# A fused attention and FFN kernel: score tiles of 32x64 without the masked quarter, and an output projection in fp16 halves scaled by a maximum that TensorE turns over

## The chip, the cores and the metric

The kernel runs on one core of a Trainium2 chip. The metric is the device time of one execution in microseconds (us), as the median of several runs. Five engines work side by side: TensorE (PE in the profile, its weight loads PEld), VectorE (DVE), ScalarE (ACT), GpSimd (POOL) and SyncE (SP), which issues the transfers.

## What is computed

x is (4, 2048, 512). Four layers stand one behind the other, each with a layernorm ahead and a residual added:

```
x = x + attention_a(layernorm(x))   # linear attention, 16 heads of 64, relu, cumulative sums
x = x + ffn(layernorm(x))           # int8-like: round rows and rhs, x @ rhs, scale back
x = x + attention_b(layernorm(x))   # gated, decaying linear attention, then layernorm
x = x + ffn(layernorm(x))           # the same rhs
```

attention_b, the second attention, is what the change is about:

```
q, k, v = x @ q_w.T, x @ k_w.T, x @ v_w.T      # 16 heads of 32; q and k then turned by rope
q_r, k_r = per head: q @ Wq[h].T, k @ Wk[h].T  # rank 16
g = sigmoid(x @ g_w.T + g_b)
M = M * decay + (g_t * k_t * scale) outer v_t  # M is 16 x 32 per head
y = q_t @ M
out = Y @ out_w.T + out_b;  hres = x + out;  layernorm(hres) * ln_g + ln_b
```

## The kernel before

The rows of x are worked in 64 chunks of 128 rows, in order. Within a chunk the recurrences are products: in attention_b the scores q·k of each pair of rows are formed, those with a key behind the query are multiplied by 0 (the mask `causals`), the rest is multiplied with v, and the state M of the chunks before is added.

Each chunk is cut into about 110 named units, each a few instructions of one engine. The table `ORDER` gives each unit a place and a lag: in slot s, every engine walks the table from top to bottom and does its own units, unit u for chunk s minus lag(u). So in one slot the units of five or six chunks stand between each other. The order is fixed in the program, an engine never skips a unit that has to wait, and units wait for each other through semaphores. The first slots are written out, the middle ones are a loop of two slots, the last are written out again (`run`, `walk`). `BANK` says which of the 8 PSUM banks a unit writes; before it writes, the unit waits until the unit that used the bank before has been read. `LATE` puts the preparation of weights into the first slots: load, maximum on DVE (`max`), turned by PE (`all`), power-of-two scale (`scale`), fp16 high half on ACT (`hi`), fp16 low half on DVE (`lo`). Semaphore counts inside the loop need registers; they are set by REGISTER_ALU instructions in the engine's own stream (`COUNTS`).

Products with fp32 accuracy are made in two ways. `three_pass` (L718 to L720) takes both operands as two fp16 halves and issues hi·hi, hi·lo, lo·hi. The others multiply fp32 tiles directly; the profile shows two MATMUL instructions for each such call. Small products use a part of the array: a product over 32 rows with 64 results takes a 32x64 tile of it, and calls that lie in different tiles can run beside each other.

The units of attention_b for one chunk, in the order of dependence: `xTb` (split and turn the normalised rows), `kb`, `qb`, `gb`, `vb` (projections), `kb_e`, `qb_e` and so on (rope, halves), `kr`, `qr` (rank products), `kr_e` (khat = kr times gate), `kT` and `kT_e` (turned, masked by head parity), `sb` (scores: L960, 16 calls, each 32 rows by 128 keys by 128 queries, 4 head groups l in 4 row groups of the array and 4 banks), `ys` (L970, q times state), `ub` (L996, state update), `sb_e0` and `sb_e1` (mask on DVE, L1434), `yb` (L983, scores times v), `y_e` (ACT copies y to SBUF, L1120), `out` (L1008, y times out_w in fp32, 4 calls of 128x128 by 512), `out_e` (L1447), `no_st`, `no_rs`, `no_ap`, `no_f` (layernorm, x3). The next chunk's `nb_ap` waits for `no_f`, since both use the tile xnb. Units of the first attention that matter here: `qk0` to `qk3` (projections, 48 fp16 matmuls each, L718 to L720), `s0`, `s1` (L800, scores in 64x64 tiles that already leave out a quarter), `so`, `o` (L818, L844), `u0`, `u1` (L863, in 128x64 tiles), `wo0`, `wo1`. The two FFNs are `mm0`, `mm1` (L891).

Of the kernel before, what the change touches and what calls it, by code (L numbers as in the profile page):

```python
# [59 lines left out]
ORDER = [("qr_e", 4), ("xhb", 4), ("sb", 4), ("ys", 4), ("mm1_e", 5), ("sb_e1", 4), ("qk2", 1), ("ub", 4), ("sb_e0", 4),  # L60
         ("mm1_a", 5), ("aT1_l", 2), ("qk1_e", 1), ("yb", 4), ("aT1_t", 2), ("u1", 2), ("y_e", 4), ("u0", 2),
         ("ub_e", 4), ("ld_t", 3), ("mm0_a", 3), ("u0_e", 2), ("nb_st", 3), ("nb_rs", 3), ("kt0", 1),
         ("bias", 2), ("u1_e", 2), ("out", 4), ("qk2_e", 1), ("wo0", 2), ("out_e", 4), ("no_st", 4),
         ("kt0_e", 1), ("wo1", 2), ("no_ap", 4), ("no_rs", 4), ("no_f", 4), ("nb_ap", 3), ("xTb_h", 3),
# [1504 lines left out]
```

## Time and profile before

| | |
|---|---|
| median of 3 runs | 3157.41 us (3151.66 to 3161.16) |
| the profiled execution | 3157.91 us, its span from first to last instruction 3156.2 us |
| PE busy | 3020.7 us, 96% |
| PEld busy | 2280.0 us, 72% |
| DVE busy | 2311.1 us, 73% |
| POOL, ACT busy | 997.9 us, 32%; 711.4 us, 23% |
| granted TensorE clock, mean | 0.987 |

The page of the profile gives for each engine its busy time, then the span in 40 slices with the busy share in tenths, then the chain of work that ended last. Views of the trace give more: the timeline lists instructions in order of time (several alike and consecutive are merged into one row with a count), the view by stretch gives the busy time of each engine between two points, the groups add up instructions of a line and shape. Matmuls are pipelined: the duration of one is a latency (0.22 us for 128 columns in fp16), and the next starts long before it ends (0.056 us later). What a matmul costs is therefore read from start to start.

### The profile page before, as it was taken

The numbers are of one execution on the slowest core, as the hardware profiler recorded it, in microseconds if no ns is written. First come the engines' busy times: TensorE is split into PE (matmuls) and PEld (weight loads), VectorE is DVE, ScalarE is ACT, GpSimd is POOL, SyncE is SP. The second block draws the span as 40 slices with busy tenths as digits, with TensorE's granted clock in tenths as the row PEclk, the third lists the DMA queues.
The fourth block names the chain that finished last, engine by engine and source line by source line (L and its number), as shares of the span: only waits on it lengthen the run. The fifth ranks groups of instructions, "written<-read, shape, count | busy, mean of one in ns | idle before, by whom it ended". The sixth has DMA issues, their size and how long they took to land.

```text
span 3156.2 us, 117197 instructions
## 1 busy us (share of the span) xinstructions
PE 3020.7 (96%) x50710; PEld 2280.0 (72%) x50836; DVE 2311.1 (73%) x5280; ACT 711.4 (23%) x1229; POOL 997.9 (32%) x1397
## 2 busy tenths in 40 slices
PE   3699999999999999999999999999999999999985
PEld 3577777777777777777777777777777777777764
DVE  6777777777777777777777777777777777777764
ACT  2222222222222222222122122222222222222211
POOL 2033333333333333333333333333333333333333
PEclk9899999999999999999999999999999999999997
DMA  4222222122222222222222222222222222222210
GB/s 169 67 41 47 45 47 51 38 48 51 37 48 51 41 44 51 42 44 50 44 47 44 44 47 45 45 46 45 45 46 46 50 40 48 50 37 48 50 34 27
DMA packets 384337, 152.96 MB, mean 48 GB/s; under 512 B 352800, under 2 KB 361632, under 8 KB 383904
## 3 DMA queue, kind: packets, MB, share of 16 engines
q1 hardware_dynamic: 383904, 146.02, 23.5%
q8 instruction: 414, 6.78, 0.9%
q14 instruction: 19, 0.16, 0.0%
HBM read 45.29 MB, written 16.78 MB: 20 GB/s over the span
## 4 chain that ended last, share of the span: by engine, by line
PE 94%; DVE 3%; DMA 1%; issue 1%; ACT 0%; POOL 0%; SPq 0%; DVEq 0%; POOLq 0%
PE bank L718 22%; PE bank L720 21%; PE bank L719 21%; PE bank L1008 7%; PE bank L891 3%; PE bank L844 3%; PE bank L800 3%; PE bank L676 3%; PE bank L960 2%; PE bank L818 2%; PE bank L863 2%; PE bank L983 2%; PE bank L970 1%; PE bank L996 1%; DVE absmax L1146 1%
## 5 line engine op out<-in xcount | busy, mean ns | idle before, releaser
L718 PE MATMUL bank<-xaT,wq_hi 128*128 128x128 f16 x2048 | 363.1, 221 | 5.0 <-DVE wk_lo L1171 4.0
L718 PE MATMUL bank<-xbT,wb 128*128 128x128 f16 x2048 | 350.7, 220 | 13.6 <-DMA xbT<-work 13.6
L719 PE MATMUL bank<-xaT,wq_hi 128*128 128x128 f16 x2048 | 362.6, 221 | 0.0
L720 PE MATMUL bank<-xaT,wq_lo 128*128 128x128 f16 x2048 | 362.6, 221 | 0.0
L718 PE MATMUL bank<-xaT,wk_hi 128*128 128x128 f16 x2048 | 360.3, 220 | 0.0
L719 PE MATMUL bank<-xaT,wk_hi 128*128 128x128 f16 x2048 | 360.1, 220 | 0.0
L720 PE MATMUL bank<-xaT,wk_lo 128*128 128x128 f16 x2048 | 360.0, 220 | 0.0
L719 PE MATMUL bank<-xbT,wb 128*128 128x128 f16 x2048 | 350.6, 220 | 0.0
L720 PE MATMUL bank<-xbT,wb 128*128 128x128 f16 x2048 | 350.6, 220 | 0.0
L638 POOL TENSOR_TENSOR work<-work 128x512 f32<-128x512 f32 x128 | 162.8, 1272 | 487.2 <-DVE work L1401 487.2
L1434 DVE TENSOR_TENSOR work<-bank,causal 128x512 f32<-128x512 f32 x256 | 159.0, 684 | 142.8 <-PE bank L960 142.8
L661 POOL TENSOR_TENSOR xf<-xwb,xf 128x512 f32<-128x512 f32 x64 | 80.9, 1264 | 528.5 <-DVE xf L1377 528.5
L1008 PE MATMUL bank<-wout,work 128*128 128x512 f32 x512 | 232.7, 597 | 1.2 <-ACT work L1120 1.2
L718 PEld LDWEIGHTS bank<-xaT,wq_hi 128*128 128x128 f16 x2048 | 202.6, 99 | 30.5 <-issue 14.7
L718 PEld LDWEIGHTS bank<-xbT,wb 128*128 128x128 f16 x2048 | 202.0, 99 | 22.2 <-DMA xbT<-work 9.8
L719 PEld LDWEIGHTS bank<-xaT,wq_hi 128*128 128x128 f16 x2048 | 202.7, 99 | 15.6
L719 PEld LDWEIGHTS bank<-xbT,wb 128*128 128x128 f16 x2048 | 202.0, 99 | 7.3
L720 PEld LDWEIGHTS bank<-xaT,wq_lo 128*128 128x128 f16 x2048 | 202.7, 99 | 0.0
L718 PEld LDWEIGHTS bank<-xaT,wk_hi 128*128 128x128 f16 x2048 | 202.0, 99 | 0.0
L720 PEld LDWEIGHTS bank<-xbT,wb 128*128 128x128 f16 x2048 | 202.0, 99 | 0.0
L719 PEld LDWEIGHTS bank<-xaT,wk_hi 128*128 128x128 f16 x2048 | 201.9, 99 | 0.0
L720 PEld LDWEIGHTS bank<-xaT,wk_lo 128*128 128x128 f16 x2048 | 201.9, 99 | 0.0
(207 smaller groups left out, 7928.1 us busy)
## 6 DMA issues: line engine op xcount, KB each, us to landing
xin<-in_L_attn_a_x SPq DMA_DIRECT2D x64, 256.0 KB, 2.6
out<-xf SPq DMA_DIRECT2D x64, 256.0 KB, 2.5
table<-in_tables SPq DMA_DIRECT2D x64, 192.5 KB, 3.0
work<-in_L_attn_a_Wq SPq DMA_DIRECT2D x1, 2048.0 KB, 8.9
work<-in_L_attn_a_Wk SPq DMA_DIRECT2D x1, 2048.0 KB, 14.4
wb<-in_L_attn_a_Wv SPq DMA_DIRECT2D x1, 2048.0 KB, 19.0
work<-in_L_attn_a_Wo SPq DMA_DIRECT2D x1, 2048.0 KB, 8.5
work<-work SPq DMA_TRANSPOSE x128, 3.1
```

What stands on the lines that cost most here:

```text
L638: pool.tensor_tensor(to[:, :, :, :], to[:, :, :, :], cross[:, :, ::-1, :], ALU.add)\
L661: pool.tensor_tensor(xf1[:, c.par, :], xwb[:, c.par, :], xf1[:, c.par, :], ALU.add)\
L676: last = nc.tensor.transpose(bank[:, i * P:(i + 1) * P], src(i), id_)
L718: nc.tensor.matmul(o, a[0], b[0], start=first, stop=False)
L719: nc.tensor.matmul(o, a[0], b[1], start=False, stop=False)
L720: return nc.tensor.matmul(o, a[1], b[0], start=False, stop=last)
L800: last = nc.tensor.matmul(bank[half_of(place), at:at + HALF], qk[half_of(p), 1, m, half_of(place)], qk[half_of(p), 0, m, half_of(q)], star ...
L818: nc.tensor.matmul(bank[half_of(place), i * VA:(i + 1) * VA], qk[half_of(p), 0, m, half_of(query_half(m, place))], state_a[half_of(p), m, ...
L844: last = nc.tensor.matmul(bank[half_of(place_q), i * VA:(i + 1) * VA], sc[g][half_of(place_k), p, i, half_of(q)], va[half_of(place_k), 2 * ...
L891: last = nc.tensor.matmul(bank[:, :], xqT[w][:, k, :], rhs_q[:, k, :], start=k == 0, stop=k == KD - 1)
L1008: last = nc.tensor.matmul(bank[:, :], yT[:, k, :], wout[:, k, :], start=k == 0, stop=k == KD - 1)
L1434: nc.vector.tensor_tensor(scb[:, l, :, :], four(bank), causals[:, 0:1, :].to_broadcast([P, 4, P]), ALU.mult).then_inc(e, 1)
```

## The change

Two things are computed otherwise, and the whole order is a new one.

1. **Scores.** `sb` forms 48 products of 32 rows by 64 keys by 64 queries (line 991 of the new kernel) in place of 16 of 32 by 128 by 128. A quarter, the keys of the second half with the queries of the first, is not formed, since the mask makes it 0. Consecutive calls go to 8 tiles of the array: 4 row groups, 2 column halves. To have equal work in both column halves, every second pair of heads keeps its key halves swapped; so `vb_e` is three ACT instructions in place of one and `kr_e` three DVE instructions in place of one, and the mask gets a second form. Columns never written are set to zero once at the start (4 more DVE memsets).
2. **Output projection.** out_w is prepared as two fp16 halves like the other weights (`load out`, `max`, `all`, `scale`, `hi`, `lo out` in slot 2) in place of one fp32 load. y is scaled by a power of two from its own largest magnitude: `y_m` (DVE: maximum of each row), `y_r` (PE: one fp32 transpose), `y_s` (DVE: five small instructions), `y_h` (ACT: high half), `y_l` (DVE: low half). `out` is 12 fp16 matmuls by 512 columns in place of 4 fp32 calls, and `out_e` scales back.
3. **Order.** All units stand in a new order, with new banks; the largest lag is 4 in place of 5. `u0` and `u1` no longer stand next to each other. PE has 41 REGISTER_ALU instructions in a loop of two slots in place of 33, DVE 38 in place of 29.

The core of the diff:

```diff
-ORDER = [("qr_e", 4), ("xhb", 4), ("sb", 4), ("ys", 4), ("mm1_e", 5), ...
+ORDER = [("nf0_st", 2), ("s0_e", 1), ("kb", 3), ("ld_x", 0), ...
...
-        wout = sb("wout", [P, KD, D])
+        wout = (sb("wout_hi", [P, KD, D], F16), sb("wout_lo", [P, KD, D], F16))
...
-                for j in range(2):
-                    for odd in range(2):
+                places = [[(j, odd, q) for j in range(2) for odd in range(2) for q in (0, 1) if q >= key_half(j, place)]
+                          for place in range(2)]
+                for n in range(6):
+                    for place in range(2):
+                        j, odd, q = places[place][n]
+                        at = tile(2 * j + odd).start + HALF * q
                         for l, (bank, f) in enumerate(four):
                             h = slice(32 * l, 32 * l + 32)
-                            last = nc.tensor.matmul(bank[:, tile(2 * j + odd)], khT[h, odd, j, :], qh[h, j, :],
-                                                    start=True, stop=True)
+                            last = nc.tensor.matmul(bank[half_of(place), at:at + HALF], khT[h, odd, j, half_of(place)],
+                                                    qh[h, j, half_of(q)], start=True, stop=True, skip_group_check=True)
...
+            def y_r(c):
+                bank, f = c.take("ym")
+                c.wait(y_reduced, c.count())
+                nc.tensor.transpose(bank[:, 0:P], y_max[:, :].to_broadcast([P, P]), ident[:, :]).then_inc(f, 1)
...
-                    last = nc.tensor.matmul(bank[:, :], yT[:, k, :], wout[:, k, :], start=k == 0, stop=k == KD - 1)
+                    last = three_pass(bank[:, :], (y_split[:, 0, k, :], y_split[:, 1, k, :]), w_part(wout, k, slice(0, D)),
+                                      k == 0, k == KD - 1)
...
+            def y_h(c):
+                c.wait(y_scaled, c.count())
+                c.filled("sb3")
+                nc.scalar.activation(y_split[:, 0, :, :], yT, ACT.Copy, scale=y_scale[:, :]).then_inc(y_hi, 1)
...
-                nc.vector.tensor_tensor(khat, bank[:, 0:HB * R], gate[:, :], ALU.mult).then_inc(khat_ready, 1)
+                nc.vector.tensor_tensor(khat[:, 0:P], bank[:, 0:P], gate[:, 0:P], ALU.mult)
+                for place in range(2):
+                    h = half_of(key_half(1, place))
+                    last = nc.vector.tensor_tensor(khat[half_of(place), P:2 * P], bank[h, P:2 * P], gate[h, P:2 * P], ALU.mult)
+                last.then_inc(khat_ready, 1)
...
+            def y_m(c):
+                c.done("y0")
+                c.done("y1")
+                nc.vector.tensor_reduce(y_max[:, :], yT.rearrange("p k t -> p (k t)"), AX_X, ALU.max,
+                                        apply_absolute_value=True).then_inc(y_reduced, 1)
+
+            def y_s(c):
+                bank, e = c.read("ym")
+                nc.vector.tensor_reduce(y_all[:, :], bank[:, 0:P], AX_X, ALU.max).then_inc(e, 1)
...
+            def y_l(c):
+                c.wait(y_scaled, c.count())
+                c.wait(y_hi, c.count())
+                nc.vector.scalar_tensor_tensor(y_split[:, 1, :, :], yT, y_scale[:, :], y_split[:, 0, :, :], ALU.mult,
+                                               ALU.subtract).then_inc(y_halved, 1)
```

PE at the scores, before. Each x counts calls; L718 to L720 are `three_pass`, L970 is `ys`.

```order
L720 MATMUL bank<-xaT,wk_lo 128x128
L188 REGISTER_ALU
L960 MATMUL bank<-work 128x128 x16
L970 MATMUL bank<-work,state_b 64x128 x8
L718 MATMUL bank<-xaT,wq_hi 128x128
```

The same place after; L745 to L747 are `three_pass`, L991 is `sb`, L1001 `ys`:

```order
L747 MATMUL bank<-xaT,wk_lo 128x128
L991 MATMUL bank<-work 64x64 x48
L1001 MATMUL bank<-work,state_b 64x128 x8
L199 REGISTER_ALU
L745 MATMUL bank<-xaT,wq_hi 128x128
```

The neighbours are the same, `qk0` ahead and `qk1` behind; 48 calls stand where 16 stood.

PE from `yb` (L983) to `out` (L1008), before:

```order
L983 MATMUL bank<-work,vbs 32x128 x16
L863 MATMUL bank<-va,work 64x65 x16
L676 MATMUL bank<-ident,work 128x128 x4
L1008 MATMUL bank<-wout,work 128x512 x4
L718 MATMUL bank<-wo_hi,work 128x512
```

The same stretch after: L1014 is `yb`, L1036 `y_r`, L890 `u1` and then `u0`, L918 `mm0`; the two gaps are the 48 matmuls of `qk2` and of `qk3`, and the third the rest of `out`:

```order
L1014 MATMUL bank<-work,vbs 32x128 x16
...
L1036 MATMUL bank<-ident,y_max 128x128
L199 REGISTER_ALU
L890 MATMUL bank<-va,work 64x65 x8
L918 MATMUL bank<-rhs_q,xqT 128x512 x4
...
L745 MATMUL bank<-wout_hi,work 128x512
...
L199 REGISTER_ALU
L890 MATMUL bank<-va,work 64x65 x8
L745 MATMUL bank<-wo_hi,work 128x512
```

`out` moved away from `yb`: two blocks of projections, `u1` and `mm0` now lie between them, and `u0`, `u1` have become two visits to the 128x64 tiles.

DVE in the same stretch, before (L1277 low half for the first attention, L1289 `qk1_e`, L1441 `ub_e`, L1331 `u0_e`):

```order
L1277 TENSOR_TENSOR work<-work 128x512
L1289 TENSOR_SCALAR work<-bank,eps_q 128x256
L1289 TENSOR_SCALAR work<-bank,eps_k 128x256
L1441 TENSOR_TENSOR u_tmp<-bank,own_head 128x128
L1331 SCALAR_TENSOR_TENSOR state_a<-state_a,keep_a,bank 128x260
```

After (L1498 `y_m`, L1492 `ub_e`, L1323 `aT0_l`, L1504 to L1514 `y_s`, L1377 `u1_e`, L1423 `mm0_e`, L1520 `y_l`):

```order
L1498 TENSOR_REDUCE y_max<-work 128x1
L1492 TENSOR_TENSOR u_tmp<-bank,own_head 128x128
L1323 TENSOR_TENSOR work<-work 128x512
L199 REGISTER_ALU
L1504 TENSOR_REDUCE y_all<-bank 128x1
L1506 TENSOR_SCALAR y_small<-y_all 128x1
L1509 TENSOR_SCALAR y_exponent<-y_small 128x1
L1512 TENSOR_SCALAR y_scale<-y_exponent 128x1
L1514 TENSOR_SCALAR y_unscale<-y_exponent,unscale 128x1
L199 REGISTER_ALU x2
L1377 SCALAR_TENSOR_TENSOR state_a<-state_a,keep_a,bank 128x260
L1423 SCALAR_TENSOR_TENSOR xf<-bank,row_scale,rs_row 128x512
```

Seven instructions came in between what stood there, and `y_l` (L1520, not shown) is the next behind the last row.

## Rows read from the trace of the kernel before

**Rows 1.** The page's first part and the PE row of the 40 slices.

```profile
PE 3020.7 (96%) x50710; PEld 2280.0 (72%) x50836; DVE 2311.1 (73%) x5280; ACT 711.4 (23%) x1229; POOL 997.9 (32%) x1397
PE   3699999999999999999999999999999999999985
```

**Rows 2.** The view by stretch: length, busy us per engine, clock.

```profile
core 0: us, PE busy (x) PEld busy (x) DVE busy (x) ACT busy (x) POOL busy (x), PEclk, DMA share, GB/s
1601.79:1648.53 46.74, 46.63 (x792) 35.26 (x795) 34.98 (x81) 10.70 (x19) 15.14 (x22) 1.00 0.26 46
55.00:110.00 55.00, 39.84 (x619) 32.13 (x616) 38.85 (x62) 11.45 (x11) 1.99 (x3) 0.83 0.25 57
110.00:160.00 50.00, 31.93 (x532) 25.41 (x533) 40.29 (x93) 11.95 (x14) 6.92 (x8) 0.83 0.31 89
```

**Rows 3.** Timeline of PE, columns start, length: `sb` of some chunks.

```profile
193.52 0.73 PE L960 MATMUL bank<-work 32*128 32x128 f32 x16
567.90 0.39 PE L960 MATMUL bank<-work 32*128 32x128 f32 x4
2964.85 0.39 PE L960 MATMUL bank<-work 32*128 32x128 f32 x4
3057.53 0.73 PE L960 MATMUL bank<-work 32*128 32x128 f32 x16 [1.02 <-ACT work L1107]
3092.32 0.94 PE L960 MATMUL bank<-work 32*128 32x128 f32 x23 [0.97 <-ACT work L1107]
3127.76 0.50 PE L960 MATMUL bank<-work 32*128 32x128 f32 x8 [0.97 <-ACT work L1107]
```

**Rows 4.** Timeline of PE: `out`, then `wo`, then `qk`.

```profile
1608.68 0.66 PE L676 MATMUL bank<-ident,work 128*128 128x128 f32 x4
1609.18 3.60 PE L1008 MATMUL bank<-wout,work 128*128 128x512 f32 x8
1612.61 0.38 PE L718 MATMUL bank<-wo_hi,work 128*128 128x512 f16 x1
1612.83 0.38 PE L719 MATMUL bank<-wo_lo,work 128*128 128x512 f16 x1
1617.79 0.22 PE L718 MATMUL bank<-xaT,wq_hi 128*128 128x128 f16 x1
```

**Rows 5.** Timeline of PE: the scores of both attentions between other work.

```profile
1648.33 0.22 PE L719 MATMUL bank<-xaT,wk_hi 128*128 128x128 f16 x1
1648.38 0.22 PE L720 MATMUL bank<-xaT,wk_lo 128*128 128x128 f16 x1
1648.53 1.17 PE L960 MATMUL bank<-work 32*128 32x128 f32 x32
1649.63 0.67 PE L970 MATMUL bank<-work,state_b 32*64 32x128 f32 x16
1650.23 0.23 PE L718 MATMUL bank<-xaT,wq_hi 128*128 128x128 f16 x1
...
1623.15 1.64 PE L800 MATMUL bank<-work 64*64 64x64 f32 x96
1624.73 0.39 PE L718 MATMUL bank<-wv_hi,xaT 128*128 128x512 f16 x1
```

**Rows 6.** Timeline of PE: `u0` and `u1` behind `yb`.

```profile
1607.60 1.15 PE L863 MATMUL bank<-va,work 128*64 128x65 f32 x32
```

**Rows 7.** Groups: mean ns of one instruction, whose prices the new ones take.

```profile
L1363 DVE TENSOR_REDUCE amax<-xf 128x1 f32<-128x512 f32 x128 | 86.8, 678 | 0.1
L1156 DVE TENSOR_REDUCE absall<-bank 128x1 f32<-128x128 f32 x10 | 2.8, 284 | 0.8 <-PE bank L683 0.6
L1159 DVE TENSOR_SCALAR exponent<-absall 128x1 uint32<-128x1 uint32 x10 | 1.5, 154 | 0.3
L1171 DVE SCALAR_TENSOR_TENSOR rankk_lo<-work,scale,rankk_hi 128x512 f16<-128x512 f32 x1 | 0.8, 752 | 0.0
L1114 ACT ACTIVATE work<-work 128x512 f16<-128x512 f32 x128 | 80.7, 630 | 278.7 <-POOL work L638 278.7
L1427 DVE TENSOR_TENSOR work<-bank,gate 128x256 f32<-128x256 f32 x64 | 27.2, 425 | 144.5 <-PE bank L720 144.4
L683 PE MATMUL bank<-ident,absmax 128*128 128x128 f32 x10 | 4.1, 410 | 62.5 <-DVE absmax L1146 62.5
```

**Rows 8.** Timeline of DVE: `o_e` of one half, the two `qb_l`/`kb_l`, `kr_e`.

```profile
1634.61 1.48 DVE L1409 TENSOR_TENSOR work<-work 128x512 f16<-128x512 f32 x1
1636.85 0.25 DVE L1310 RECIPROCAL recip_d<-bank 128x4 f32<-128x4 f32 x2 [0.77 <-PE bank L844]
...
1638.92 0.90 DVE L1409 TENSOR_TENSOR work<-work 128x512 f16<-128x512 f32 x1
...
1644.20 0.42 DVE L1427 TENSOR_TENSOR work<-bank,gate 128x256 f32<-128x256 f32 x1 [2.30 <-PE bank L720]
```

**Rows 9.** Timeline, the last chunk: from `yb` to the last result.

```profile
3133.06 0.81 ACT L1120 ACTIVATE work<-bank 128x256 f32<-128x256 f32 x2 [5.40 <-PE bank L983]
3134.02 4.23 PE L1008 MATMUL bank<-wout,work 128*128 128x512 f32 x8 [0.57 <-ACT work L1120]
3138.29 0.69 DVE L1447 TENSOR_TENSOR xnb<-bank,xnb 128x512 f32<-128x512 f32 x1 [6.59 <-PE bank L1008]
```

More of the change, by code:

```diff
@@ L56 @@
 MAGIC = 1.5 * 2.0 ** 23
[L60 to L64, printed above, removed]
[4 rows of a table removed]
-         ("s1_e", 1), ("gb", 3), ("v1_e", 1), ("kb_e", 3), ("ub_a", 4), ("kb_a", 3), ("qb_e", 3), ("kb_h", 3),
[5 rows of a table removed]
+ORDER = [("nf0_st", 2), ("s0_e", 1), ("kb", 3), ("ld_x", 0), ("nf0_rs", 2), ("nf1_q", 4), ("na_st", 0), ("s1_e", 1),
+         ("na_rs", 0), ("kb_e", 3), ("na_ap", 0), ("v0_e", 1), ("nf0_ap", 2), ("v1_e", 1), ("rnd1", 4),
+         ("qb", 3), ("qb_e", 3), ("xTa_h", 0), ("ub_a", 4), ("kb_a", 3), ("kb_h", 3), ("gb", 3), ("xTa_l", 0),
[3 rows of a table added]
+         ("o0_e", 1), ("qr_e", 3), ("nf0_q", 2), ("kT_e", 3), ("vb_e", 3), ("qT1_t", 4), ("xTa_t", 0),
+         ("aT0_h", 1), ("qk0", 0), ("sb", 3), ("aT1_l", 1), ("sb_e1", 3), ("ys", 3), ("qk1", 0), ("sb_e0", 3),
+         ("mm1", 4), ("ub", 3), ("qk0_e", 0), ("xhb", 3), ("yb", 3), ("qk2", 0), ("rnd0", 2), ("y_e", 3),
+         ("mm1_e", 4), ("qk1_e", 0), ("y_m", 3), ("ub_e", 3), ("aT0_l", 1), ("y_r", 3), ("y_s", 3),
+         ("qT0_t", 2), ("y_h", 3), ("mm1_a", 4), ("u1", 1), ("u1_e", 1), ("ld_t", 2), ("st_o", 4), ("mm0", 2),
+         ("mm0_e", 2), ("mm0_a", 2), ("y_l", 3), ("qk3", 0), ("qk2_e", 0), ("bias", 1), ("qk3_e", 0),
+         ("nb_st", 2), ("nb_rs", 2), ("aT0_t", 1), ("out", 3), ("u0", 1), ("out_e", 3), ("no_st", 3),
+         ("no_rs", 3), ("u0_e", 1), ("no_ap", 3), ("no_f", 3), ("nb_ap", 2), ("aT1_t", 1), ("wo0", 1),
+         ("xTb_h", 2), ("wo1", 1), ("nf1_st", 3), ("v0", 0), ("xTb_l", 2), ("xTb_t", 2), ("wo_e", 1), ("s0", 0),
+         ("nf1_rs", 3), ("s1", 0), ("kt0", 0), ("v1", 0), ("nf1_ap", 3)]
 LAG = dict(ORDER)
@@ L102 @@
 LATE = {
[L103 to L114 removed]
[10 rows of a table removed]
[L125 to L138 removed]
+    (0, "nf0_st"): ("load o",),
+    (0, "qk0_e"): ("max o",),
+    (0, "qk1_e"): ("turn decay",),
+    (0, "qk2_e"): ("all o", "keep decay"),
+    (0, "no_st"): ("scale o", "hi o"),
+    (1, "gb_s"): ("lo o", "load rhs", "load bk"),
+    (1, "ys"): ("max rhs", "all rhs"),
+    (1, "mm1_e"): ("columns of rhs", "rows of rhs"),
+    (1, "qk1_e"): ("scale rhs",),
+    (1, "y_h"): ("max bk", "all bk"),
+    (1, "qk2_e"): ("scale bk", "hi bk"),
+    (1, "xTb_h"): ("round rhs", "load bq"),
+    (1, "wo_e"): ("lo bk", "load g", "load rk", "load rq"),
+    (2, "nf1_q"): ("max bq", "all bq"),
+    (2, "nf0_ap"): ("scale bq", "hi bq"),
+    (2, "ub_a"): ("max g", "all g"),
[8 rows of a table added]
+    (2, "aT0_t"): ("max out", "all out"),
+    (2, "no_st"): ("scale out", "hi out"),
+    (2, "xTb_l"): ("lo out",),
+}
+TAKEN = ("q", "k", "v", "o", "rhs", "bk", "bq", "g", "bv", "rk", "rq", "out")
+BORROWED = {"decay": (0, "qk1_e", 0),
+            "o": (0, "qk2_e", 2),
+            "rhs": (1, "ys", 3),
+            "rhs rows": (1, "mm1_e", 6),
+            "bk": (1, "y_h", 7),
+            "bq": (2, "nf1_q", 7),
+            "g": (2, "ub_a", 7),
+            "bv": (2, "qr", 4),
+            "rk": (2, "ys", 6),
+            "rq": (2, "mm1_e", 7),
+            "out": (2, "aT0_t", 4)}
 def borrowed_before(bank, slot, place):
@@ L1099, in vb_e @@
                 c.filled("ub", 1)
-                nc.scalar.activation(vbs[:, :], bank[:, :], ACT.Copy, scale=unscale[:, SBV:SBV + 1]).then_inc(e, 1)
+                one = unscale[:, SBV:SBV + 1]
+                nc.scalar.activation(vbs[:, 0:256], bank[:, 0:256], ACT.Copy, scale=one)
+                for place in range(2):
+                    h = half_of(key_half(1, place))
+                    last = nc.scalar.activation(vbs[half_of(place), 256:512], bank[h, 256:512], ACT.Copy, scale=one[h, :])
+                last.then_inc(e, 1)
             def kT_e(c):
@@ L1492, in _ @@
                           qb_l=turned_l("q", turn_q, q_halves), kb_l=turned_l("k", turn_k, k_halves),
-                          gb_e=gb_e, qr_e=qr_e, kr_e=kr_e, sb_e0=sb_e(0), sb_e1=sb_e(1), ub_e=ub_e, out_e=out_e,
+                          gb_e=gb_e, qr_e=qr_e, kr_e=kr_e, sb_e0=sb_e(0), sb_e1=sb_e(1), ub_e=ub_e, y_m=y_m, y_s=y_s,
+                          y_l=y_l, out_e=out_e,
                           no_st=no_st, no_ap=no_ap, no_f=no_f, nf1_st=nf1_st, nf1_ap=nf1_ap, nf1_q=to_int(1),
```

124 lines of the change are left out of this document (66 added, 58 removed), and 48 rows, old and new, of tables (COUNTS, LATE, ORDER).

## The prediction

> **What bounds the kernel now.** I read the page's busy times first: PE 96%, DVE 73%, and PE at 9 in nearly every slice [rows 1]. The view by stretch over one whole chunk shows why nothing else matters there: of 46.74 us PE is busy 46.63 at full clock, DVE 34.98, ACT 10.70, POOL 15.14 [rows 2]. So in the middle a chunk costs what PE's list costs from start to start. The starts of the scores give the period [rows 3]: from 567.90 to 2964.85 us lie 51 chunks, 47.00 us each; in the written-out part, 193.52 to 567.90, 8 chunks at 46.80. The loop with its 33 register instructions per two chunks thus costs 0.2 us a chunk more. The last intervals are 35.44 and 34.79 us with PE waiting for ACT, and from the last scores to the end it is 28.4 us: there the chain of one chunk is the bound, not PE's work. In the profiled execution 61 intervals are bound by PE, two and the tail by the chain, and 193.5 us lie ahead of the first scores.
>
> **The change part by part, on PE, per chunk.**
>
> Output projection. `out` takes 1612.61 - 1609.18 = 3.43 us for its 8 instructions [rows 4]. The 24 fp16 matmuls by 512 of `wo` take 1617.79 - 1612.61 = 5.18, so 12 take 2.59. **-0.84 us**, the safest term: same array shape, same columns.
>
> Scores. The 32 instructions of `sb` take 1649.63 - 1648.53 = 1.10 us [rows 5]. The new unit has 96 instructions of half the columns, on 8 tiles of the array in turn. No row shows 8 tiles. The nearest is L800, 64 columns on 4 tiles: 96 instructions in 1624.73 - 1623.15 = 1.58 us, way out included, 66 ns for four. If eight tiles run beside each other as those four do, it is 12 rounds of 66 ns = 0.79 us, -0.31. The step from `sb` to `ys` is now one without a change of shape; I take 0.04 for it, **-0.35** together. Bounds: -0.45 if the rounds keep to less and the shape change saves 0.1; and +0.48 if only four run beside each other and 96 cost 1.58. I take the first since the four tiles of L800 are also two row groups by two column halves, and the four of L960 are four row groups in four banks: both ways of running side by side are in the trace, and the new unit joins them.
>
> L800 spends 16.5 ns per instruction, L960 itself 34 (1.10 / 32). The Trainium skill (TensorE: Matmul & The Clock Gate, "Wait — 56ns, not 53.3ns?") says that the start of one matmul follows that of another by about 25 ns at least, however few the columns. By that page 96 instructions would take 2.4 us, where my sum has 0.79. L800's 16.5 ns speak against the page as a rule for tiles.
>
> Visits to tile shapes. `u0` and `u1` took 1608.68 - 1607.60 = 1.08 us in one visit straight behind `yb` [rows 4, 6]. Now each stands alone among 128x128 products. Entering a small shape costs 1648.53 - 1648.38 = 0.15 where the step would be 0.056 [rows 5], 0.09 more; leaving costs about as much again. Two entries and one more exit, the one entry from `yb` kept as an exit: **+0.33**, bounds +0.15 (one pair) and +0.5.
>
> `y_r` is one more fp32 transpose. Four of them take 1609.18 - 1608.68 = 0.50 [rows 4]: **+0.12**.
>
> Register instructions, 41 for 33 per two chunks: 0.2 us for 33/2 gives 0.012 each, **+0.05**.
>
> **The other engines.** DVE gets `y_m` 0.678, `y_s` 0.284 + 4 x 0.154 = 0.90, `y_l` 0.752, 0.06 more in `out_e`, and `kr_e` in three pieces: I take 0.28 each (0.284 for 128 columns), 0.85 for 0.425 [rows 7]. Together +2.8, so 37.8 us of 46. ACT gets `y_h` 0.63 and about 0.5 for `vb_e` in three pieces, of 46. Both hide behind PE as totals, and what decides is the order.
>
> Chain of y. Between `yb` and `out` PE now has `qk2` 48 x 0.056 = 2.7, `y_r` 0.12, `u1` 0.7, `mm0` 0.86, `qk3` 2.7: 7.1 us. `y_r` has to start 2.7 after `yb`; `y_e` (0.81) [rows 9] and `y_m` (0.68) with the hand-overs need 1.7. From `y_r`: latency 0.41, `y_s` to the scale 0.75, `y_h` 0.63, `y_l` 0.75, and DVE has `u1_e` and `mm0_e` (0.48, 0.74) ahead of `y_l`. `mm0` ends 4.4 after `yb`; 0.2 latency, `mm0_e`, `y_l` end at 6.1. PE wants it at 7.1. Hidden, with 1 us to spare; if DVE is later than that, each us is a us per chunk.
>
> Queue at `kr_e`. From the end of `ob1` PE has `ob0`, `kt1`, `kr`, `vb` (0.4 + 0.5 + 0.67 + 2.59 = 4.2) until `qr`, which waits for `qb_l`, and 4.8 until `kT`, which waits for `kr_e`. DVE has `o1_e`, 1638.92 - 1636.85 = 2.07, then `qb_l` at 0.90 or 1.48, then `kr_e` 0.85 [rows 8]: 3.0 to 3.6, then 3.8 to 4.4. That leaves 0.4 at the least, if DVE has come to `o1_e` in time. Before, DVE waited 2.30 us for PE at `kr_e`; this cover is what shrinks. I put **+0.03** for a wait now and then.
>
> The weights of `out` cost DVE some 5.5 us in slot 2, and the four memsets fall in the wait for the first load.
>
> Sum for a chunk: -0.84 - 0.35 + 0.33 + 0.12 + 0.05 + 0.03 = -0.66. I take **-0.68**, halfway to what `sb` gives if its rounds are a little shorter. Times 61: **-41 us**.
>
> **Start and end.** At the end the chain counts whole. Per pass it gains `y_m` 0.68, `y_r` 0.41, `y_s` 0.75, `y_h` 0.63, `y_l` 0.75, five hand-overs 0.3 and 0.45 at `kr_e`: 4.0; it loses 0.84 and 0.35 at PE: +2.8. `out` of the last chunk ran at half speed (4.23 us from 3134.02) [rows 9]; longer pauses of PE may add such stretches. Two intervals and the tail, 3 x 2.8 = 8.4, with the clock **+10**, bounds +4 and +16. At the start neither PE (71.8 of 105 us) nor DVE (79.1) is full [rows 2], the pieces are placed anew, 5.5 us of DVE come in, and a chunk's way to its scores is 3.0 slots in place of 3.1: **+1**, bounds -10 and +12, since no row prices a new order.
>
> The profiled execution was 3157.91 us, its span 3156.2: 3157.9 - 41 + 10 + 1 = 3127.9. The median lies 0.5 below that execution: **3127 us**.
>
> **The rivals.**
>
> A. Eight tiles run no faster than four. `sb` then costs 1.58 us, 0.79 more than taken: +0.11 per chunk, +7 in the middle, +13 at the ends: 3178 us, slower. It decides from 1.3 us for the 96 on (+0.5 a chunk), where the gain is used up. For it: no row has 8 tiles, and the two instructions of a call go to the same tile, so that eight tiles are busy only if twice as many calls are in flight. Against: L960 does a round of four tiles with 128 columns in 0.14 us, L800 one with 64 in 0.066: where the tiles differ, columns set the pace, not the number of calls.
>
> B. DVE comes late at `kr_e` or `y_l` and PE waits. For it: of DVE's 11.8 us of idle time a chunk 3.5 go, more chained small instructions, and only 0.4 us to spare. Against: totals of 38 in 46. A wait of 0.6 us a chunk costs 37: 3164 us; from 0.5 on the gain is gone.
>
> C. The pace of `sb` is set by the number of its instructions and stays at L960's 34 ns: 96 take 3.3 us, 2.5 more than taken, 64 x 2.5 = +160: 3287 us. L800 with its 16.5 ns is the row against it. The floor of the skill's page named above is the same kind of rule; by its figure the time would be some 3230 us.
>
> D. The start or the end loses more: the chain waits at the cold clock, weights come late. +16 on my terms: 3143 us.
>
> E. The change saves the quarter in name only, because the products that remain bring as many rounds as before: 12 rounds for 8 would be so if a round took 92 ns. Then -0.35 becomes 0, 64 x 0.35 = +22: 3149 us.
>
> **How the numbers follow.** My forecast 0.60, A 0.12, B 0.15, C 0.03, D 0.06, E 0.04. A measurement of this kernel can tell 0.3%, 9.5 us, from no change: faster means under 3148, slower over 3167. Faster: 0.60, D 0.05, a third of B 0.05, a quarter of E 0.01: 0.71. Slower: A 0.10, C 0.03, B 0.04: 0.17. The rest, 0.12, is within. The range starts at 3106, with the low bounds of `sb` (-6), the visits (-8) and the start (-7), and ends at 3168, which takes in B's price and leaves out A, C and B's tail, about 0.2.
>
> **What the profile after would show.** The new `out` should be 12 starts at 0.216 us. The scores should take 0.8 us from their first start to `ys`; 1.6 is A, 3.3 is C. The period between two starts of the scores should be 46.3 in the loop. PE should have no wait at `qr`, `kT`, `y_r` or the first matmul of `out`; a wait in the group of these lines, with DVE as releaser, is B. The last intervals should be 38 us. I am wrong as a whole if PE is no longer busy 99% in the middle.

## The result, and the profile after it

The changed kernel takes **3179.21 us** (median of 4 runs, 3177.79 to 3181.84), the kernel before 3157.84 in the same comparison (3151.66 to 3161.16): 1.0074 of it, with a 95% interval of 1.0061 to 1.0087. Forecast were 3127 us and a range up to 3168: wrong in sign and outside the range. The profiled execution of the changed kernel lasted 3181.84 us, its span is 3180.1.

The page after it, first part, PE's 40 slices and the queue that carries instructions (before: 3156.2 us span, PE and DVE as in [rows 1], and 6.78 MB of instructions in 414 packets):

```profile
PE 3020.7 (95%) x55253; PEld 2263.4 (71%) x55253; DVE 2566.8 (81%) x5867; ACT 784.3 (25%) x1422; POOL 1075.7 (34%) x1398
PE   3699999999999999999999999999999999999985
q8 instruction: 473, 7.75, 1.0%
```

PE is busy exactly as long as before, and the slices tell nothing. The view by stretch over two chunks in a row, from scores to scores, tells more (columns as in [rows 2]):

```profile
1606.41:1654.07 47.66, 46.82 (x866) 35.01 (x864) 38.79 (x91) 11.81 (x23) 16.53 (x21) 1.00 0.25 45
1559.79:1606.41 46.62, 46.61 (x866) 35.04 (x864) 38.79 (x91) 11.81 (x23) 16.53 (x21) 1.00 0.22 46
```

Two chunks make one pass of the loop. The chunk in which the loop closes takes 1.04 us more than the other, and PE isn't busy in 0.84 of it. That is one fault. The other chunk is full, at 46.62 us where the forecast had 46.3: that is a second one, and it doesn't show as idle time of PE.

By starts of the scores: the 61 intervals of the middle are 2874.9 us for 2864.0 before (+10.9, forecast -41), the first start 194.9 for 193.5, the last two intervals 39.85 and 38.69 for 34.80 and 35.44 [rows 3], the tail 31.7 for 28.4. Start and ends together +13, forecast +11. So the miss of 52 us lies in the middle. DVE is busy 38.79 us of a chunk where 37.8 were forecast.

What PE waits for, view of the waits, the changed kernel:

```profile
engine line waited for: us in total, times, longest us
PE bank L745 <- issue: 24.0, 28, 1.2
PE bank L745 <- DMA xbT<-work: 13.6, 2, 9.2
PE bank L745 <- DVE work L1520: 7.1, 3, 2.8
PE bank L1036 <- DVE y_max L1498: 4.0, 3, 1.4
```

The first line is new: "issue" is time in which PE waited for nothing that the profile shows. Its place is `kb`, the first product of each pass of the loop, and 26 of the 28 are the loop's closings. The timeline there, the last product of `v1` and the first of `kb`:

```profile
1635.48 0.38 PE L746 MATMUL bank<-wv_lo,xaT 128*128 128x512 f16 x1
1635.70 0.38 PE L747 MATMUL bank<-wv_hi,xaT 128*128 128x512 f16 x1
1636.91 0.23 PE L745 MATMUL bank<-xbT,wb 128*128 128x128 f16 x1 [0.83 <-issue]
```

1.21 us from start to start where 0.216 would do. The view of the loop's line shows why (durations of the branch in ns: least, median, most). Before, L448, and after, L472:

```profile
L448 PEldq COMPARE_BRANCH  x26: 88/352/406, 660.4 to 3010.5; - x26
```

```profile
L472 PEldq COMPARE_BRANCH  x27: 88/3610/3903, 594.2 to 3050.6; - x27
```

The branch that closes the loop on PE takes ten times as long. It starts at 1632.95, 2.75 us ahead of the last queued matmul, so the queue hides most of it. And 1 us after it starts, one packet of instructions arrives; the DMA view of 1633.8 to 1635.2 us:

```profile
DMA packets 1, 0.02 MB, mean 12 GB/s; under 512 B 0, under 2 KB 0, under 8 KB 0
q8 instruction: 1, 0.02, 5.1%
```

Two theories stood at this point, beside the prediction's own pricing. **Supply**: PE's program comes in pieces of 16 KB while it runs (7.75 MB in 473 packets), and the changed kernel's branch stands badly in its piece. **Size**: the loop grew (3528 instructions on PE's queues for 3249, counted in the traces, each matmul with its weight load as two; 41 register instructions for 33), and a larger loop costs more.

### The profile page after: what moved, and what is told of

Its sections match the earlier page's. It is cut to its first block, busy times and chain, and to the rows that moved or that the text cites. A ratio compares the mean times of both kernels' runs of the same rounds, so it can differ in the third digit from the quotient of the medians.

```text
span 3180.1 us, 127626 instructions
## 1 busy us (share of the span) xinstructions
PE 3020.7 (95%) x55253; PEld 2263.4 (71%) x55253; DVE 2566.8 (81%) x5867; ACT 784.3 (25%) x1422; POOL 1075.7 (34%) x1398
## 3 DMA queue, kind: packets, MB, share of 16 engines
q8 instruction: 473, 7.75, 1.0%
## 4 chain that ended last, share of the span: by engine, by line
PE 93%; DVE 3%; issue 2%; DMA 1%; ACT 0%; SPq 0%; POOL 0%; POOLq 0%; DVEq 0%; ACTq 0%
PE bank L745 24%; PE bank L747 23%; PE bank L746 23%; PE bank L918 4%; PE bank L827 3%; PE bank L703 3%; PE bank L871 3%; PE bank L890 2%; PE bank L991 2%; PE bank L845 2%; PE bank L1014 2%; PE bank L1001 1%; PE bank L1027 1%; DVE absmax L1192 1%; DMA work<-in_L_attn_a_Wk 0%
## 5 line engine op out<-in xcount | busy, mean ns | idle before, releaser
L745 PE MATMUL bank<-xbT,wb 128*128 128x128 f16 x2048 | 350.6, 220 | 36.6 <-issue 23.1
L745 PE MATMUL bank<-xaT,wq_hi 128*128 128x128 f16 x2048 | 362.8, 221 | 17.2 <-DMA xaT<-xa_split 12.4
L747 PE MATMUL bank<-xaT,wq_lo 128*128 128x128 f16 x2048 | 361.6, 221 | 1.6 <-issue 1.6
L745 PE MATMUL bank<-xaT,wk_hi 128*128 128x128 f16 x2048 | 358.9, 220 | 0.0
L747 PE MATMUL bank<-xaT,wk_lo 128*128 128x128 f16 x2048 | 358.5, 220 | 0.0
L747 PE MATMUL bank<-xbT,wb 128*128 128x128 f16 x2048 | 350.3, 220 | 0.0
L665 POOL TENSOR_TENSOR work<-work 128x512 f32<-128x512 f32 x128 | 201.8, 1576 | 312.1 <-DVE work L1447 312.1
L745 PEld LDWEIGHTS bank<-xbT,wb 128*128 128x128 f16 x2048 | 201.8, 99 | 54.5 <-issue 50.3
L745 PEld LDWEIGHTS bank<-xaT,wq_hi 128*128 128x128 f16 x2048 | 201.9, 99 | 49.8 <-issue 41.8
L652 POOL TENSOR_TENSOR xwb<-xwa,xf 128x512 f32<-128x512 f32 x64 | 108.5, 1695 | 325.2 <-DVE xf L1423 325.2
L1445 DVE TENSOR_TENSOR work<-bank,table 128x512 f32<-128x512 f32 x128 | 87.7, 685 | 160.6 <-PE bank L747 160.6
L747 PEld LDWEIGHTS bank<-xaT,wq_lo 128*128 128x128 f16 x2048 | 202.4, 99 | 0.0
L747 PEld LDWEIGHTS bank<-xbT,wb 128*128 128x128 f16 x2048 | 201.9, 99 | 0.0
L745 PEld LDWEIGHTS bank<-xaT,wk_hi 128*128 128x128 f16 x2048 | 201.5, 98 | 0.0
```

The costliest lines, as they stand in the source:

```text
L652: pool.tensor_tensor(xwb[:, c.par, :], xwa[:, :], xf0[:, :], ALU.add).then_inc(x2_ready, 1)
L665: pool.tensor_tensor(to[:, :, :, :], to[:, :, :, :], cross[:, :, ::-1, :], ALU.add)\
L745: nc.tensor.matmul(o, a[0], b[0], start=first, stop=False)
L747: return nc.tensor.matmul(o, a[1], b[0], start=False, stop=last)
L1445: nc.vector.tensor_tensor(to[:, :, :, :].rearrange("p j e t -> p (j e) t"), four(bank), cos[:, None, :].to_broadcast([P, 4, P]), ALU.mult)
```

## Experiments

### The same instructions at other addresses

The edit, with another number each time; nothing that any engine computes is touched:

```
-with nc.Fori(FIRST_LOOP_SLOT // 2, CHUNKS // 2, engines=[eng.engine], hint_back_edge=True) as it:
+with nc.Fori(FIRST_LOOP_SLOT // 2, CHUNKS // 2, engines=[eng.engine], hint_back_edge=True,
+             head_slot={eng.engine: 0} if name_of == "PE" else None) as it:
```

It pads ahead of the loop until the loop's first instruction stands at that place, called slot here and in what follows, of a block of 256 instructions. It has nothing to do with the slots of `ORDER`.

> The changed kernel, its work untouched; only the place of PE's loop in the instruction stream is set: the loop's first instruction stands in slot 0 of a fetch block of 256 instructions, so that the closing branch (3528 instructions in the loop body, counted in the trace) falls in slot 199. Theory (the back edge): in the changed kernel PE's closing branch takes 3.3 to 3.9 us at 26 of 27 times, and a 16 KB transfer of instructions starts 1 us after the branch does, while the kernel before has 0.35 us there; the branch now stands so near a block's edge that the loop's first block isn't fetched in time. Then this kernel's branch takes 0.35 us, the step from v1 to kb falls from 1.1 us to about 0.25, and the time is 3179 - 26 x 0.85 = 3157 us (3153 to 3161). Rival 1: the edge costs what it does because the loop has 8 more register instructions and 280 more instructions in all; then nothing changes, 3179. Rival 2: what is given back at the edge is lost again to a wait for DVE elsewhere in the chunk, as DVE sets the period: branch 0.35 us, but 3170 us or more.

> The same with the loop's first instruction in slot 60, so that the branch stands in slot 3 of a block. Theory of the back edge: PE comes into the branch's block only 3 instructions ahead of it, so the fetch is late as in the changed kernel: branch 3.3 to 3.9 us, step from v1 to kb 1.1 us, 3179 us. Rival 1 (size of the loop alone): 3179 too, as for every slot. If the fetch doesn't depend on the slot of the branch but on something else in the block, 0.35 us.

> The same with the loop's first instruction in slot 100, the branch in slot 43. If the fetch of the loop's first block starts when PE enters the branch's block, 43 instructions are 21 matmuls of 512 columns at 0.216 us, 4.5 us ahead of the branch by the clock, as much as a fetch takes (3.3 to 3.9): branch 0.35 us and 3157 us. If the fetch needs a whole block ahead, or starts only with the branch: 3.6 us and 3179 us.

> The kernel before, its work untouched, with the loop's first instruction of PE in slot 84; its body has 3249 instructions, so the branch stands in slot 4 of a block. Theory of the back edge: the branch takes 3.3 to 3.9 us in place of 0.35. PE has only 0.9 us of short matmuls queued there, and its wait ahead of the scores grows by 2.5 to 3.2 us per edge: 3158 + 26 x 2.8 = 3231 us (3220 to 3242). Rival (the size of the changed loop is the cause, and the place means nothing): 3158 us.

Measured: slot 0 **3204.5 us** (1.0138, 1.0121 to 1.0155), slot 60 3205.8, slot 100 3165.5 (one run each), and the kernel before at slot 84 **3252.8** (1.0292, 1.0275 to 1.0309). The kernel before, its work untouched, is 3% slower by its address, and in slot 0 the larger loop closes with a short branch: size as the cause is out. But of the four expectations none has its time. Slot 0, which should have been the cure, was 25 us worse than the changed kernel, slot 60 was 27 us over its 3179, and the kernel before at slot 84 was 22 over its 3231. Slot 100 fell between its two sides, with a branch of 2.94 us in the median. The waits, slot 0, slot 60, and the kernel before at slot 84:

```profile
PE bank L871 <- issue: 47.5, 39, 1.7
PE bank L745 <- issue: 2.5, 9, 0.5
```

```profile
PE bank L745 <- issue: 23.5, 29, 1.2
PE bank L747 <- issue: 18.6, 24, 1.3
```

```profile
PE bank L960 <- issue: 82.4, 25, 3.7
```

In slot 0 the branch is cured (median 448 ns, and 24 us at L745 are down to 2.5), but PE now stands still at L871, in the middle of straight code. Slot 60 has the branch's wait and a second one in the `qk` behind the scores. At slot 84 PE pauses 3.3 us at nearly every closing, and the pauses cost twice: between 200 and 3000 us the granted clock is at its lower level, 1.2 GHz, for 72 us in all, in short stretches behind the pauses. At slot 40, further down, it is there for none, and the means are 0.975 and 0.987.

The view also has a wait for issue of 10 us in 63 or 64 times at L918 for slots 0, 60 and 100. That one isn't real: one record of the four products is missing there, and from the product ahead to the one behind the time is the same as at slot 144, 1.51 us a chunk. The timeline of slot 0 at L871:

```profile
1704.31 1.16 PE L845 MATMUL bank<-state_a,work 64*64 64x65 f32 x64
1705.29 1.60 PE L871 MATMUL bank<-va,work 64*64 64x65 f32 x90
1708.59 0.34 PE L871 MATMUL bank<-va,work 64*64 64x65 f32 x6 [1.70 <-issue]
```

PE runs through 154 products with their weight loads, 308 instructions, in 2.6 us; then nothing for 1.7 us. A packet of instructions arrives from 1706.23 to 1707.18, and PE goes on 1.4 us later. That is the supply theory in a wider form: not only the branch can wait for a piece, straight code can too, where PE uses one up faster than the next comes. How long one takes shows at the branch: 3.3 to 3.9 us where it has to be fetched. The Trainium skill (Runtime: NRT & Kernel Launch, "Instruction fetch mechanics") gives the block as 256 instructions and says that a taken branch out of the fetched window stalls; the changed kernel's trace agrees, 3.6 us, while the branch of the kernel before, which goes back as far and has the same `hint_back_edge`, takes 0.35. It also says that in straight code the fetch is hidden by the pace of issue; the 47.5 us at L871 show otherwise.

> The changed kernel, its work untouched, PE's loop with its first instruction in slot 144 of a fetch block, the branch in slot 87. Theory (instruction supply): PE fetches its program in pieces of 16 KB, 256 instructions, one piece ahead, and one takes some 3.6 us from the request to the next instruction, as the branch that has to fetch shows; PE stands still where it runs through 256 instructions in less than that, queue of some 0.9 to 2.6 us aside. In the trace with slot 100 the times between every 256th instruction, shifted to slot 144, are 3.4 us and more everywhere inside the loop, against 1.9 with slot 0 (stall of 1.9 us among the products of the first attention) and 2.5 with slot 60. So here there is no stall at all: no step over 0.45 us in the products, the branch at most 2.7 us, hidden behind v1's 2.6 us, and 3157 us (3153 to 3161). Rival: slot 100 with its 3165 us was the best there is, since the branch costs 2.6 us or more unless it stands in the last quarter of a block: 3165 to 3180.

Measured **3157.5 us** (3154.95 to 3161.76; 1.0007 of the kernel before, 0.9998 to 1.0017), as the theory had it. The branch takes 2.64 us in the median and hides behind `v1` but for 0.10 us (0.320 from start to start on the mean at a closing, for 0.216); the waits for issue are down to 3.1 us in all:

```profile
PE bank L872 <- issue: 1.9, 2, 1.2
PE bank L746 <- issue: 1.2, 4, 0.5
```

21.7 of the 52 us of the miss are the address of the changed kernel's loop.

> The kernel before with PE's loop at slot 40: by the count in its trace the branch (slot 216) then comes 6.6 us after the block's edge, and no block of 256 instructions is run through in under 3.2 us. Theory of instruction supply: the stalls of the kernel before go, 0.13 us a chunk ahead of and in the scores and 3 us in all at the products of the first attention: 3155 - 9 = 3146 (3143 to 3151). Rival (the kernel before has no supply stalls; its 47.0 us a chunk in the loop are register instructions): 3155.

> The kernel before with PE's loop at slot 0. The branch (slot 176) is early enough, 5.5 us after its block's edge, so that it costs nothing. But one block of 256 instructions (the 1024th to the 1280th, all among the first attention's products of 65 columns) is run through in 1.88 us. Theory of instruction supply: a stall of 1.5 us or more there in each pass of the loop, 26 x 1.6 = 42 us more than slot 40: 3188 (3180 to 3200). Rival (only the place of the branch counts): as slot 40, 3146.

Measured: slot 40 **3149.4 us** (0.9977, 0.9967 to 0.9986), near the 3146 expected: the kernel before also lost some 8 us to its address, which the prediction had put down to register instructions. Slot 0: 3159.8 (one run), where 3188 was expected: **a miss**. Where the expectation has a piece that PE uses up in 1.88 us, among the products of L845, no pause of 1.5 us or more shows: the waits for issue at L845 are 3.3 us in 8 times. The products do take 1.61 us a chunk for 1.45 at slot 40, which is most of the 10 us by which this run lies over slot 40. The timeline there:

```profile
1730.95 0.27 PE L720 MATMUL bank<-wg_lo,xbT 128*128 128x256 f16 x1
1731.06 0.27 PE L721 MATMUL bank<-wg_hi,xbT 128*128 128x256 f16 x1
1731.26 0.70 PE L819 MATMUL bank<-state_a,work 64*64 64x65 f32 x32
```

The likely reason is PE's queue. By the two closing branches it holds 13 to 17 matmuls: the branch of the kernel before starts 0.93 us ahead of the last queued one with products of 0.056, that of the changed kernel 2.75 us ahead with products of 0.216. Instructions leave their piece that much earlier than they run. The piece begins, by the count behind the expectation, some six products before 1731.26. With 16 products of 0.109 ahead it was opened up to 1.7 us earlier, and 1.7 + 1.88 is what a fetch takes. In slot 0 of the changed kernel the piece opens inside the products of 15 ns, where 16 are worth 0.25 us.

This form was found from the miss, and no run was made to test it. Nor do the traces settle it: no record holds its instruction's address, and the length of a piece comes out otherwise by how the instructions are counted off. Counted 16 products ahead, with the register instructions put at one place or another, the shortest piece of the kernel before in slot 0 is 3.4 or 1.9 us, that of slot 100 is 3.9 or 2.5, that of the kernel before at slot 84 1.9 or 3.8. What the runs show is that the address decides, and that slots 144 and 40 leave almost no wait.

### The scores

> The changed kernel with the scores of before: four tiles of 32x128, the evictions of kr, vb and the scores as before; order, banks and the output projection stay changed. PE's loop starts in slot 48, where by the same count no piece of 256 instructions is run through too fast (body 3272 instructions). Theory: the new scores save PE 0.05 us a chunk and cost DVE 0.45 us at kr_e, on which PE waits: 0.16 us at kT and 0.12 at qr. Undoing them gives the 0.16 at kT back and costs 0.05: 0.1 us a chunk less than the changed kernel at a good slot, 3157 - 7 = 3150 (3144 to 3156). Rival (the prediction's pricing, new scores save 0.35 us a chunk): 3157 + 21 = 3178.

> The kernel before with the new scores alone (96 products in 32x64 tiles, khat and v in three pieces, the mask), order, banks and fp32 output projection as before; PE's loop starts in slot 8 (body 3505 instructions). DVE waited 2.3 us for PE at kr_e, so its 0.45 us more are hidden. Theory: the scores take 1.05 us in place of 1.10: 3158 - 3 = 3155, with up to 5 us more since the first 248 instructions of the loop, now with 192 of the scores among them, take 2.75 us only (3150 to 3163). Rival (the prediction's pricing of the scores, -0.35 us a chunk): 3158 - 22 = 3136.

The edit of the first puts `sb`, `kr_e`, `vb_e` and `sb_e` back; of the second, the other way round. Each also sets the loop's slot, 48 and 8. Of the first, cut to the lines on PE:

```
-for n in range(6): for place in range(2): ... half_of(place), at:at + HALF ... half_of(q)
+for j in range(2): for odd in range(2):   ... bank[:, tile(2 * j + odd)], khT[h, odd, j, :], qh[h, j, :]
```

Measured: the changed kernel with the old scores **3139.2 us** (0.9954, 0.9938 to 0.9971), the kernel before with the new ones **3159.4** (1.0015, 1.0005 to 1.0024). Both expectations chose the side against the prediction's -0.35, and both times it was that side, but the sizes differ: the old scores gain 18 us over slot 144, not 7, and the kernel before with the new ones is at the upper end of its 3150 to 3163. From start to start, read from the traces (us; the first column medians, the others means):

```
                                  last qk -> first qk   vb -> qr   qr -> kT   chunk in the loop
before, slot 40                   1.852                 0.216      0.056      46.81
before with new scores, slot 8    1.796                 0.216      0.056      46.94
changed with old scores, slot 48  1.851                 0.304      0.056      46.51
changed, slot 144                 1.796                 0.332      0.223      46.80
```

"last qk -> first qk" is the whole block of scores with its ways in and out, "vb -> qr" and "qr -> kT" are single steps in which PE may wait for DVE. By the medians the new form saves 0.055 us, in both kernels. By the means it doesn't in the changed kernel: over the loop the block takes 1.866 us at slot 144 and 1.851 with the old scores, since one chunk of two at slot 144 has small delays between the products (1.94 for 1.80). In the kernel before the block falls from 1.95 to 1.90, but its 128 further instructions a chunk come with new waits right behind the scores: `L722 <- issue` 3.5 us in 11 times, and the q products of the first attention take 5.33 us a chunk for 5.15. Ahead of the scores the wait for issue is 6.7 us for 2.3, most of it where the loop is entered and left. So it ends 10 us over slot 40.

The 96 products follow each other at 10.9 ns (1.036 us from the first start to the last), and `ys` starts 0.98 us after the first of them. The changed kernel:

```profile
1653.75 0.22 PE L747 MATMUL bank<-xaT,wk_lo 128*128 128x128 f16 x1
1654.07 1.19 PE L991 MATMUL bank<-work 32*64 32x64 f32 x92
1655.04 0.29 PE L1001 MATMUL bank<-work,state_b 32*64 32x128 f32 x1
```

> The changed kernel at slot 144 with only the first 32 of each 64 columns in the 96 products of the second attention's scores: half of the scores are left out, all instructions stay. Theory (the pace of the 96 products, 10.6 ns each, is the pace at which instructions come to the array, not the array's work): still 10.6 ns each, 1.02 us for the 96, and the time of slot 144. Rival (eight tiles work on 64 columns for 85 ns a round): with 32 columns a round takes about half, 0.5 us for the 96, and 30 us less in all.

Measured 3154.7 us (one run; half of the scores are left out). In a chunk without a pause the scores read

```profile
1594.38 1.26 PE L992 MATMUL bank<-work 32*64 32x32 f32 x91
```

and the median from first to last start is 0.957 us with 32 columns, 1.036 with 64. Half the columns buy 8%. So the columns do not set the pace. What remains is a cost that each product has whatever its columns, and the natural reading is the pace at which instructions come to the array; no run varied that by itself. Three times as many products at 0.37 of the interval (32 took 0.90 us) give nearly the old time.

### DVE and the waits of 0.1 us

The middle columns of the table are the other part. The view of the waits doesn't list them: each is too small. DVE's and POOL's timelines of the changed kernel, from `nf0_ap` to `kr_e`:

```profile
1641.18 0.54 DVE L1308 TENSOR_SCALAR xna<-xin,mean_var_a,rstd_a 128x512 f32<-128x512 f32 x1
1641.64 1.50 DVE L1308 TENSOR_SCALAR xf<-xwa,mean_var_f,rstd_f 128x512 f32<-128x512 f32 x1
...
1644.85 1.76 DVE L1455 TENSOR_TENSOR work<-work 128x512 f16<-128x512 f32 x1
...
1648.98 1.05 DVE L1455 TENSOR_TENSOR work<-work 128x512 f16<-128x512 f32 x1
1650.07 0.29 DVE L1473 TENSOR_TENSOR work<-bank,gate 128x128 f32<-128x128 f32 x1
1650.37 0.59 DVE L1476 TENSOR_TENSOR work<-bank,gate 64x128 f32<-64x128 f32 x2
```

```profile
1641.35 1.50 POOL L665 TENSOR_TENSOR work<-work 128x512 f32<-128x512 f32 x1 [3.72 <-DVE work L1447]
1644.41 1.65 POOL L665 TENSOR_TENSOR work<-work 128x512 f32<-128x512 f32 x1 [1.56 <-DVE work L1447]
...
1648.21 1.27 POOL L660 TENSOR_TENSOR xwb<-xwb,lnb_row 128x512 f32<-128x512 f32 x1
```

No DVE line has a bracket: it runs without a pause. `qb_l` ends at 1650.03 and PE's `qr` starts at 1650.18; `kr_e` ends at 1650.96 and `kT` starts at 1651.02. Three instructions of DVE are stretched beside POOL. The same forms take 0.54 (`xna`) and, in the kernel before with POOL idle, 0.69; here they take 1.50, 1.76 and 1.05. All three start while POOL is already at work on 512 columns and end only after it: 1643.14 for POOL's 1642.85, 1646.61 for 1646.06, 1650.03 for 1649.48. `xna`, which started ahead of POOL, keeps its 0.54. So it looks as if the later one waits for the earlier; by no means every DVE instruction beside POOL is stretched, and no run sorted out which are.

> The changed kernel with PE's loop at slot 144 and one step of DVE moved: nf0_ap (the first norm's output for the feed-forward of the first layer, 0.54 us, but 1.50 us where it stands, beside a POOL addition) goes ahead of kb_e, where DVE idles 1.9 us for PE. Nothing else changes; PE's list is the same. Theory: the steps of 0.22 us from qr to kT and of 0.33 from vb to qr (0.056 and 0.216 in the kernel before) are waits for DVE, which runs without a pause from kb_e to kr_e; with 0.5 to 1.5 us less there they go: 61 x 0.28 = 17 us less than slot 144's 3157.5, so 3141 (3138 to 3146). Rival: the steps belong to the small pieces themselves or to the hand-over, or DVE is held by something other than its own queue: unchanged, 3157.

> The kernel with the old scores at slot 48 (3139.2 us) and the same move of nf0_ap. There qr follows vb by 0.30 us on the mean in place of 0.216 and kT has no wait. Theory: 61 x 0.09 = 5 us less, 3134 (3131 to 3138), which beats both kernels by more than 0.5%. If DVE's relief does nothing: 3139. If the new scores pay once DVE isn't late, this kernel is not faster than the one with the new scores and the move: by the block of scores (1.796 for 1.851 us) the new ones then save 0.055 a chunk, 3 us.

```
-... ("na_rs", 0), ("kb_e", 3), ("na_ap", 0), ("v0_e", 1), ("nf0_ap", 2), ("v1_e", 1), ...
+... ("na_rs", 0), ("nf0_ap", 2), ("kb_e", 3), ("na_ap", 0), ("v0_e", 1), ("v1_e", 1), ...
```

The preparation of one weight that hung on `nf0_ap` in an early slot goes to `v0_e`; the loops stand at slots 144 and 48.

Measured: **3138.7 us** with the new scores (0.9943, 0.9927 to 0.9960), **3132.9** with the old (0.9927, 0.9911 to 0.9944), the fastest of all. `vb` to `qr` is 0.216 and `qr` to `kT` 0.056 in both. The group of the moved step in the changed kernel, and with the move:

```profile
L1308 DVE TENSOR_SCALAR xf<-xwa,mean_var_f,rstd_f 128x512 f32<-128x512 f32 x64 | 92.8, 1450 | 0.0
```

```profile
L1308 DVE TENSOR_SCALAR xf<-xwa,mean_var_f,rstd_f 128x512 f32<-128x512 f32 x64 | 34.5, 540 | 0.0
```

58 us of DVE's time go, and the chunk falls from 46.80 to 46.46 us, 0.34 for the 0.28 of the two waits; 0.05 more lie between the transposes of `kT` (0.93 to 0.88). With that relief the new scores no longer cost 18 us, but 6. And 4 of these are not theirs: at slot 144 the closing branch still takes 2.66 us, and the step to `kb` is 0.36 us there for 0.216 at slot 48, 27 times. So what the new scores cost once DVE isn't late is about 2 us, too little to tell from nothing with two different addresses. A gain like the forecast 0.35 us a chunk, 21 us, is ruled out.

## Why the prediction was wrong

**What bounds the kernel.** Right about PE, wrong about one thing in it: "the loop with its 33 register instructions costs 0.2 us a chunk more". At slot 40 the same instructions take 46.81 for 46.99 a chunk. In the written-out part the same chunks take 46.79. So the 0.2 were supply, and the register instructions cost nothing that shows.

**Output projection, -0.84.** Right: 12 starts of 0.216 (1667.80 to 1670.17 and one step), 2.59 for 3.43 us.

**Scores, -0.35.** The step that failed. Four tiles at 66 ns a round were taken to mean eight tiles at 66: 12 rounds, 0.79 us. Measured is a round of 86 ns (1.036 us for 12), and the block saves 0.055 us by the median and, at slot 144, nothing by the mean. Rival E was nearest: it named 92 ns as the round at which the term is 0. Rival A (eight tiles run no faster than four, 1.58 us) was too dear, but the sentence against it, that "columns set the pace, not the number of calls", is what the run with half the columns refutes. Rival C, a pace set by the number of instructions, had the kind of cause that this run points to, with 34 ns where 10.9 were measured. And the pieces that the new form costs `kr_e` were priced on DVE only as a chance of 0.03: together, taken out again, the new scores cost 0.29 us a chunk at these addresses (46.80 - 46.51). Some 0.25 of it are waits for DVE (0.17 at `kT`, 0.05 between its transposes, 0.03 at `qr`) and 0.05 the closing branch at slot 144.

**Visits, `y_r`, registers, +0.50.** Right as a sum. With the old scores and both kernels at a good address the rest of the change is 46.51 - 46.81 = -0.30 us a chunk, where the steps without the scores gave -0.84 + 0.33 + 0.12 + 0.05 + 0.03 = -0.31. That it fits to 0.01 is partly luck: 0.09 us of wait at `qr` are in the 46.51, and with `nf0_ap` moved the rest is 46.38 - 46.81 = -0.43. The single terms were not measured one by one.

**DVE, +0.03.** Too small: `kr_e` was seen as the place, with 0.4 us to spare "if DVE has come to `o1_e` in time". It hadn't, and the margin was counted with durations from moments without POOL. The two waits are 0.28 us a chunk, 0.20 of them by the new scores (0.168 at `kT`, 0.03 at `qr`). Rival B named mechanism and place, with 0.6 us for its price. DVE's added work was also counted as 2.8 us where it is 3.8, 0.9 of them the stretched `nf0_ap`.

**Start and ends, +11.** Right: +13.

**Address of the loop.** In no step. 21.7 us on the changed kernel. The kernel before had lost 8 as well, which the forecast took over as a cost of both: net +13.7.

The sum closes: scores 0.29 instead of -0.35 a chunk, 0.64 x 61 = 39 us, and 13.7 of address make 53 for a miss of 52. Two things make it less exact than it looks: 0.05 of the 0.29 are the closing branch once more, and the times come from several sets of runs, each with the kernel before beside it. By the ratios to that kernel, 21.7, 8 and 18 read 21, 7 and 17. The sign that the prediction named for its failing as a whole, PE no longer busy 99% in the middle, shows in one chunk of two (46.82 of 47.66).

So of what the change does, the output projection with its order is worth 10 us net at good addresses (3139.2 for 3149.4, 7 by the ratios): 20 in the middle, less its price at the ends. The new scores cost 18 as the order stands, 3 of them by the closing branch at slot 144, and 6 with DVE relieved, 4 of them by that branch.

## What to carry to other kernels

Where PE is the bound, count its instructions, not only its matmul time: a stretch in which 256 of them pass in less than the 3.3 to 3.9 us of a fetch can stall when a block begins there (slot 0 of the changed kernel did, slot 0 of the kernel before hardly), and any edit of a loop of thousands of instructions moves all blocks. So compare two versions of a long loop only with the loop's first instruction put in a slot chosen for each, and read "issue" waits (with the counts beside them, as a missing record looks like a wait) and the closing branch's duration before a difference under 2% is put down to the edit. Splitting work into smaller tiles pays only until the cost of a product no longer falls with its columns (here 10.9 ns for 64, 10.1 for 32); below that, count the pieces that it costs the evictions, and count them on the engine's timeline with the durations that stand at that very place.

## What the runs showed that was not expected

- The address of a loop alone moved the changed kernel between 3157.5 and 3205.8 us and the kernel before between 3149.4 and 3252.8.
- A fetch of one block takes 3.3 to 3.9 us, by the closing branch where it has to wait, of which the packet itself is mostly 0.9 to 1.4.
- Pauses of 3.3 us at the closing bring 72 us of lower clock with them (kernel before, slot 84).
- PE's products in tiles follow each other at 10.9 ns with 64 columns and 10.1 with 32, each with its weight load.
- A DVE pass of 0.54 us took 1.50 when it started behind a POOL addition, and ended after it; one that started ahead kept its 0.54. POOL's addition took 1.50 to 1.65 for a mean of 1.27 in the kernel before.
- What stays open: why PE's 96 products run at just that pace, and exactly which pieces PE waits for. The form of the supply rule with the queue was made to fit a miss, not tried on a new address. What the new scores are worth with DVE relieved and the closing branch short was not run either.
